# A decoder's first attention stage, with layer 0's values projected tile by tile inside the loop over heads instead of ahead of it

## The reference

```python
x = _layernorm(x + _L0_attn_ref(x, Wg, bg, Wv, bv, Wo, bo))
# in _L0_attn_ref, with H = 16 heads of 16 columns
g = x @ Wg.T + bg
v = x @ Wv.T + bv
attn = _genetic_fitness(g)          # cosine of g's rows, causal mask, fitness, softmax
out = einsum('bhij,bhjd->bhid', attn, v)
return out @ Wo.T + bo
```

## Time and profile before

| | us |
|---|---|
| median of 3 runs (lowest, highest) | 2650.11 (2647.54, 2652.91) |
| the profiled execution's own time | 2642.07 |
| its span | 2640.2 |
| first stage: projection, to its last VectorE operation | 0 to 79.8 |
| first stage: heads, first instruction to that of the next stage | 80.4 to 495.2 |

### The profile page before, as it was taken

How to read it: one execution, slowest core, us unless ns; L and a number is a source line. 1 busy time by engine, 2 the same in 40 slices (tenths; PEclk the granted TensorE clock), 3 DMA queues, 4 the chain that set the end, 5 groups by cost and what they waited for, 6 DMA issues and landing times. The chain is left out here.

```text
span 2640.2 us, 44590 instructions
## 1 busy us (share of the span) xinstructions
PE 2322.6 (88%) x17186; PEld 1783.3 (68%) x17186; DVE 1347.6 (51%) x2515; ACT 1131.5 (43%) x1934; POOL 845.9 (32%) x881
## 2 busy tenths in 40 slices
PE   9688888699998778698989869999999699999994
PEld 4567767466665555565666557888888588888893
DVE  5588878378887671002353536778778311111113
ACT  1466666355565554343333315555655111111113
POOL 2355545144444481000010113445444212212221
PEclk9699999799999898899999989999999799999997
DMA  2244435310120559574112031333332566665564
GB/s 76 79 103 121 122 102 131 92 33 25 31 67 17 182 195 225 128 210 136 32 32 64 24 130 54 111 113 101 99 120 91 216 203 181 180 198 173 183 223 140
DMA packets 212481, 313.23 MB, mean 119 GB/s; under 512 B 63792, under 2 KB 194736, under 8 KB 198960
## 3 DMA queue, kind: packets, MB, share of 16 engines
q1 hardware_dynamic: 190416, 255.25, 31.4%
q0 software_dynamic: 13440, 17.90, 3.7%
q10 hardware_dynamic: 8416, 37.23, 3.7%
HBM read 188.88 MB, written 121.45 MB: 118 GB/s over the span
## 5 line engine op out<-in xcount | busy, mean ns | idle before, releaser
L2653 ACT ACTIVATE me_h<-me_ps_h 128x512 f32<-128x512 f32 (+1 forms) x160 | 88.7, 554 | 423.8 <-PE me_ps_h L2631 423.8
L2694 DVE TENSOR_SCALAR me_yo<-me_ps_y,moe_xg 128x256 f32<-128x256 f32 x72 | 34.9, 484 | 422.8 <-PE me_ps_y L2641 369.1
L2567 POOL DMA_INDIRECT xo<-me_yo,me_row x72 | 112.7, 1565 | 410.2 <-DVE me_yo L2694 349.2
L2631 PE MATMUL me_ps_h<-me_xt,me_w 128*128 128x256 f32 (+1 forms) x1056 | 210.0, 357 | 0.0
L2641 PE MATMUL me_ps_y<-me_w,me_h 128*128 128x256 f32 x944 | 209.2, 379 | 0.7 <-DVE me_yo L2694 0.7
L2076 POOL TENSOR_TENSOR l1x_e<-l1x_e,l1x_ri 128x1024 f32<-128x1024 f32 x64 | 121.7, 1901 | 235.5 <-DVE l1x_ri L2360 235.5
L2641 PEld LDWEIGHTS me_ps_y<-me_w,me_h 128*128 128x128 f32 x944 | 179.0, 190 | 24.8 <-issue 1.1
L2631 PEld LDWEIGHTS me_ps_h<-me_xt,me_w 128*128 128x128 f32 x1056 | 182.0, 191 | 20.0
L664 POOL TENSOR_TENSOR l0x_e<-l0x_e,l0x_ri 128x1024 f32<-128x1024 f32 x64 | 120.0, 1896 | 202.7 <-DVE l0x_ri L893 202.7
L2195 PE MATMUL l1x_ps_p<-l1x_xct,l1x_w_q 128*128 128x256 f32 x512 | 122.3, 383 | 0.3 <-ACT l1x_xct L2281 0.3
L2233 PE MATMUL l1x_ps_o<-l1x_w_o,l1x_ot 128*128 128x256 f32 x512 | 118.8, 385 | 1.4 <-ACT l1x_ot L2306 1.4
(11 more groups left out here) (421 smaller groups left out, 5543.7 us busy)
## 6 DMA issues: line engine op xcount, KB each, us to landing
me_w<-in_w SPq DMA_DIRECT2D x33, 2048.0 KB, 9.6
xs<-dec_zero SPq DMA_DIRECT2D x31, 1032.0 KB, 6.9
k<-kv_kt ACTq DMA_DIRECT2D x16, 1024.0 KB, 6.4
v<-kv_va ACTq DMA_DIRECT2D x16, 1024.0 KB, 5.8
l1x_kt<-k SPq DMA_DIRECT2D x16, 1024.0 KB, 5.0
l1x_va<-v SPq DMA_DIRECT2D x16, 1024.0 KB, 5.7
moe_w_first<-in_w SPq DMA_DIRECT2D x7, 2048.0 KB, 9.9
moe_xg<-xs SPq DMA_DIRECT2D x32, 258.0 KB, 2.8
```

Of the source, the lines that this page charges most:

```text
L2567: pool.indirect_dma_start(token_rows, bass.IndirectOffsetOnAxis(row[:, j % 2, q:q + 1], 0), yo[:, j % 2, q, :], None, compute_op=ALU.add). ...
L2631: last = pe.matmul(ps_h[i % HB][:, f % 2, 0:P * size(j)], weights(j)[:, FFN * c + f * P:FFN * c + f * P + P], xt[:, j % 2, c, 0:P * size(j ...
L2653: act.activation(h[:, j % 2, 2 * i:2 * i + 2, 0:P * size(j)], ps_h[i % HB][:, :, 0:P * size(j)], ACT.Gelu).then_inc(gelued, 1)
```

## The change

The projection makes g alone: a product 256 columns wide (`ps_g`), and no v. x has four buffers instead of two. The reciprocal of the sums of squares is taken in four parts of eight tiles, three of them among the tiles; the logarithm comes ahead of the square root. The masks, the identity in bf16 and the padded tiles' memsets move from the start of the heads into the projection's block, where GpSimd and ScalarE do them ahead of the first tile.

The heads make v per tile. TensorE transposes x (`transpose_x`) and multiplies by Wv (`project_v`) in `ps_a[1]`, ScalarE copies between the two (`copy_xv`), VectorE adds the bias (`add_v`) into `va`, which now has four slots. The second half of the next tile's `transposes` waits for `add_v`, since both use `ps_a[1]`. The four weights and biases are waited for together. x has five slots, since `bias_x` moves two steps back; `roots` and `normalise` move one step back, and the lists of GpSimd and ScalarE are cut at another place. SP still stores tile n - 8 in its turn n.

```diff
 # l0_attn_project, VectorE and ScalarE
-                    dve.tensor_tensor(gv[:, n, :], ps_gv[n % 2][:, 0:D], bias[:, 0:D], ALU.add).then_inc(g_biased, 1)
-                    dve.tensor_tensor(va[:, n, :, 0:3:2, :],
...
+                    dve.tensor_tensor(gv[:, n, :], ps_g[n % 2][:, :], bias[:, :], ALU.add).then_inc(g_biased, 1)
...
+                def invert(k):
+                    at = slice(CHUNK * k, CHUNK * k + CHUNK)
+                    dve.wait_ge(summed, CHUNK * k + CHUNK)
+                    dve.tensor_scalar(lo[:, at, :], n2[:, at, :], 2.0 ** -115, None, ALU.max).then_inc(floored, 1)
+                    item_done(dve, floored, k)
+                    dve.reciprocal(inv[:, at, :], lo[:, at, :]).then_inc(inverted, 1)
...
-                unrolled(TILES, [(0, add_bias), (1, sum_squares)])
+                unrolled(TILES, [(0, add_bias), (1, sum_squares), (2, last_of_chunk)])
...
 # l0_attn_heads, SyncE
+                sp.dma_start(w_v[:, :, :], wgv.rearrange("(k p) n -> p k n", p=P)[:, :, D:2 * D]).then_inc(w_loaded, 16)
+                sp.dma_start(b_v[:, :], bcast(bgv[D:2 * D])).then_inc(w_loaded, 16)
...
-                    slot_free(sp, x_biased, n, 2)
-                    sp.dma_start(x[:, n % 2, :], x_in[n, :, :]).then_inc(x_loaded[n % 2], 16)
+                    slot_free(sp, x_biased, n, XR)
+                    slot_free(sp, xv_ready, n, XR)
+                    sp.dma_start(x[:, n % XR, :], x_in[n, :, :]).then_inc(x_loaded[n % XR], 16)
 # VectorE
+                def add_v(n):
...
+                    item_done(dve, v_ready, n)
+                    slot_free(dve, applied, n, VR)
+                    dve.tensor_tensor(va[:, n % VR, :, 0:3:2, :], ps_a[1][:, 2:4, :].rearrange("p a b -> p (a b)").rearrange("p (j a d) -> p j a d", a=2, d=HD),
...
 # TensorE
+                def transpose_x(n):
+                    item_done(pe, x_loaded[n % XR], n // XR, 16)
+                    item_done(pe, ops_copied, n, 2)
+                    slot_free(pe, v_biased, n, 1)
+                    for k in range(2):
+                        last = pe.transpose(ps_a[1][:, k, :], x[:, n % XR, k * P:(k + 1) * P], ident[:, :])
+                    last.then_inc(xv_ready, 1)
+
+                def project_v(n):
...
+                    item_done(pe, xv_copied, n)
+                    for k in range(2):
+                        last = pe.matmul(ps_a[1][:, 2:4, :].rearrange("p a b -> p (a b)"), xvt[:, n % 2, k * P:(k + 1) * P], w_v[:, k, :],
+                                         start=k == 0, stop=k == 1)
+                    last.then_inc(v_ready, 1)
...
+                            slot_free(pe, v_biased, n, 1)
 # ScalarE
+                def copy_xv(n):
+                    item_done(act, xv_ready, n)
+                    slot_free(act, v_ready, n, 2)
+                    act.activation(xvt[:, n % 2, :], ps_a[1][:, 0:2, :].rearrange("p a b -> p (a b)"), ACT.Copy).then_inc(xv_copied, 1)
...
-                walk([(0, copy_ops), (2, lambda n: exponentials(n, 1)), (0, lambda n: guard(n, 0)), (7, normalise), (2, copy_et), (0, lambda n: guard(n, 1)), (1, lambda n: exponentials(n, 0))])
+                walk([(8, normalise), (2, lambda n: exponentials(n, 1)), (0, lambda n: guard(n, 0)), (0, copy_xv), (2, copy_et), (0, lambda n: guard(n, 1)), (1, lambda n: exponentials(n, 0)), (-1, copy_ops)])
```

More of the change, by code:

```diff
@@ L225, in _ @@
                 identity_f32(nc, pool, ident, made)
+                pool.memset(after[:, :], 0.0).then_inc(cleared, 1)
+                pool.wait_ge(cleared, 1)
+                pool.affine_select(out=after[:, :], in_=after[:, :], compare_op=ALU.is_ge, fill=-1e30, base=0,
+                                   pattern=[[-1, P]], channel_multiplier=1).then_inc(after_cut, 1)
+                pool.memset(lpad[:, :, :, :], 0.0).then_inc(cleared, 1)
+                pool.memset(rpad[:, :, :, :], 0.0).then_inc(cleared, 1)
+                pool.wait_ge(cleared, 3)
+                pool.memset(lpad[:, :, :, HD + 1:HD + 2], 1.0).then_inc(one_set, 1)
+                pool.memset(rpad[:, :, :, HD:HD + 1], 1.0).then_inc(one_set, 1)
                 def square(n):
@@ L278, in l0_attn_heads @@
          applied, inverted, divided, multiplied, x_biased, residual_done, stats_done, mv_done, ln_step, ln_done, normed) = (kit.sem(n) for n in names)
[L279 removed]
+        x_loaded = [kit.sem(f"x_loaded{b}") for b in range(XR)]
         stored = [kit.sem(f"stored{t}") for t in range(G)]
@@ L303, in _ @@
                 pool.memset(on3[:, 1, :], 0.0).then_inc(parted, 1)
-                pool.memset(after[:, :], 0.0).then_inc(cleared, 1)
                 pool.memset(half[:, :], -0.5).then_inc(set_, 1)
@@ L444, in residual @@
                     dve.bn_aggr(mv[:, g % 2, t, :], stats[:, n % 2, :]).then_inc(mv_done, 1)
-                walk([(1, weigh_even), (0, lambda n: correlate(n, 1)), (2, divide), (0, row_sums), (2, residual), (-1, lambda n: correlate(n, 0)), (0, fitness)])
+                walk([(1, weigh_even), (0, add_v), (0, lambda n: correlate(n, 1)), (2, divide), (0, row_sums), (2, residual), (-1, lambda n: correlate(n, 0)), (0, fitness)])
             @block.tensor
             def _(pe):
-                pe.wait_ge(identb_set, 1)
-                pe.wait_ge(guard_set, 1)
                 pe.wait_ge(set_, 4)
+                def transpose_x(n):
[6 more added lines that the diff above has]
+                def project_v(n):
+                    if n == 0:
+                        pe.wait_ge(w_loaded, 64)
+                    item_done(pe, xv_copied, n)
[3 more added lines that the diff above has]
+                    last.then_inc(v_ready, 1)
                 def transposes(n):
@@ L527, in multiply @@
                     last.then_inc(multiplied, 1)
[L528 removed]
+                walk([(3, multiply), (0, transpose_x), (2, lambda n: transpose_e(n, 0)), (0, project_v), (2, lambda n: transpose_e(n, 1)), (1, sum_inverse), (2, lambda n: transpose_e(n, 2)), (2, lambda n: transpose_e(n, 3)), (0, lambda n: score(n, 1)), (2, apply), (-1, transposes), (-1, lambda n: score(n, 0))])
             @block.scalar
             def _(act):
[L532 to L534 removed]
+                def copy_xv(n):
+                    item_done(act, xv_ready, n)
+                    slot_free(act, v_ready, n, 2)
+                    act.activation(xvt[:, n % 2, :], ps_a[1][:, 0:2, :].rearrange("p a b -> p (a b)"), ACT.Copy).then_inc(xv_copied, 1)
                 def copy_ops(n):
```

132 lines of the change are left out of this document (67 added, 65 removed).

## The result

The changed kernel takes 2607.94 us (4 runs, 2606.00 to 2614.71), the kernel before on the same chip 2651.51 (2647.54 to 2654.84): ratio 0.9841, 95% interval 0.9818 to 0.9864. (The ratios here weigh all runs, so they are not quite the quotient of two medians; differences are those of the medians.) Two later comparisons gave 0.9838 [0.9815, 0.9861] and 0.9866 [0.9832, 0.9900], with medians 39.6 and 37.0 us apart. The profiled execution took 2609.12 us, its span is 2605.9.

A forecast was written before the change was run, and what follows sets the result against it. TensorE was taken to bound the projection; in the heads no engine was full and two chains closed the step. Terms -27.4 - 3.8 - 2.3 + 1 + 3 = -29.5 us, from the runs' median 2650.1, gave 2620.6; range 2611 to 2635.

The forecast's parts named there:

- The projection: Projection stage: tiles 1.08 us apart on TensorE with 256-column records, first product shorter, reciprocal parts costing 1; -27.4 us.
- The numbers for all tiles: Last addition to the heads' first instruction: reciprocal leaves the path, net one operation less; -3.8 us, bounds -3.3 and -4.2.
- The set-up: Start of the heads to TensorE's first transpose: memsets and mask move to the projection; -2.3 us, between 0 and -3.6.
- A full step: Each step of the heads: the new work on v fits under existing work; +0.04 us a step, +1 over 31.
- the product takes the place of the hole: Heads' step: `project_v` fills TensorE's idle time before 206.80, and the work between second and fourth quarter fits with 0.15 to spare.
- the two signs of being wrong in the steps: Heads: the prediction is wrong if a step exceeds 11.8 us, or if TensorE waits for `xvt`.
- The first steps: Heads' first three steps, at half clock: new work costs between 0 and 7.6 us, taken as +3.
- The pauses: Pauses without a releaser, as one of 2.95 us at 342.47: may come once more or less, 3 to 5 us.
- In part: Rival, heads: 0.2 to 0.9 us of the new 1.08 appear in each step; 2626 to 2648 us, chance 0.18.
- TensorE as the bound: Rival, heads: all 1.08 us are paid in each of 31 steps; 2653 us, no change, chance 0.04.
- the falling clock: Rival, projection: TensorE granted 1.2 GHz, 33 us more; 2654 us, no change, chance 0.03.
- late x: Rival, heads: x lands late behind the zeros, TensorE stands 2.4 us in each of 24 steps; 2678 us, chance 0.02.

## Why the prediction missed

**The projection, -27.4.** Measured -26.57. The additions were 1.08 us apart with the clock at 1.00, as worked out; the first of all (not among the lines above) came at 8.48 instead of 11.05 us, 2.6 sooner where 1.7 were counted, and the three parts of the reciprocal cost about 0.5 us each, where 1 in all was. **The numbers for all tiles, -3.8**: -3.94. **The set-up, -2.3**: -2.48. These three carried the forecast and were right.

**A full step, +0.04, +1 in all.** The step "the product takes the place of the hole" was right in kind and mis-sized: +0.19, about +5. The chain was the right one (`multiply`, `guard`, copy, product, second quarter). But in the heads four records of 256 columns follow each other in 0.97 us, not 0.86. In the changed kernel this is 196.90 - 195.93, and in before it stood between 204.59 and this row:

```profile
205.56 0.60 PE L498 MATMUL l0ah_ps_e<-l0a_ident,l0ah_e 128*128 128x128 f32 x4
```

And the copy lets the product start 1.82 us behind `multiply`, not 1.76: 0.06 + 0.11 = 0.17 more. The rate of another stage was taken for this one, though a row of this very product stood in the timeline. By the product made twice no cover is left: the next microsecond costs a microsecond. Of the two signs of being wrong in the steps, one did not come (a step over 11.8 us) and one did: TensorE waited for `xvt`. Its weight loads for the product did so 31 times between 50 and 470 us, for 10.0 us in all.

**The first steps, +3.** The two first profiles say -2.5, but over all profiled executions the stretch took 39.7 to 44.2 us with before's steps and 40.9 to 45.5 with the changed ones (without the doubled product), by when the clock rose and whether a pause fell in it. The term is small and its sign open.

**The pauses, "may come once more or less: 3 to 5 us, in the range", and "on the median of the runs, 8 us higher for the same program".** These are the step that failed, and they are one: pauses taken for an accident that both kernels share. In before they are no accident of 3 us. Eight places in the heads are exposed, each costs 2.4 to 5 us when it is hit, and moving them away is worth 15 to 18 us. The profiled execution had two such pauses, the second one with six had a span 10.2 us longer, and the 8 us by which the median lay over the profile were taken over to the changed kernel as they stood. The changed kernel has one or two pauses in its profiles, and its median lies 1.2 us under its profiled time. So of the 12.7 us between the forecast of 2620.6 and 2607.94, 8.0 + 1.2 = 9.2 are this step; the other 3.5 are the terms (profiled times 2642.07 - 2609.12 = 33.0 us apart, where 29.5 were forecast), and these hold the two pauses of before's profile too.

What took most of the pauses away, as the runs point to it, was in the change all along: its five slots of x and its new order send the zeros at another time in the step, away from TensorE's dense run. The forecast followed SyncE's order only to see whether x would be late. The new step of 357 instructions, by which the boundaries wander, is not needed for it, since the kernel without the work on v has 342 and no pause. What is left in the changed kernel falls on the zeros again, at 1473 and once at 11457.

How large this is stays rough. On one chip moving the boundaries gives 15.24 us in before and 9.56 in the changed kernel, so 5.7 by the medians and 7.8 by the means; resampling the runs puts the latter anywhere from 3 to 13. The earlier trace rows showed one pause; a second stood at 381.1 us and exactly 1024 instructions behind it, which the trace of before would have told.

**The sum.** With the pauses moved away in both kernels the change is worth 31.3 us on one chip (29.4 by the means), and 28.4 by two chips (2629.43 - 2601.02), where 29.5 were forecast. That it comes so near is in part luck, for the full step was 4 us worse than counted and the first steps some 5 better in the first profiles. Before's medians in the comparisons were 2651.51, 2646.79, 2647.03, 2642.70 and 2648.53. Its runs spread by 15 to 28 us within each of the later ones, a width that the pauses can make. What sets the level from chip to chip stays open.

**The rivals.** "In part" was true with 0.15 us a step, just under its 0.2. TensorE as the bound, the falling clock and late x did not come: x was waited for twice, 1.1 us in all.

## What to carry to other kernels

A pause that ends with nothing but "issue" deserves a count: number the instructions of its engine up to each pause, and if they agree modulo a block, the instruction fetch is late there. Two things have to meet for it: a block boundary at the end of a dense run, and a big transfer beside that run. A step whose length, times a small number, is near a multiple of that block puts the boundary at the same place of every such step; some instructions ahead move it away. Another order, or one more buffer, moves the transfer, and this can happen without being meant: so a change of slots or of a list's order is to be asked what it does to the big transfers. A product's time is to be taken from a row in the stage where it will stand, and when it fills a hole to the last tenth, the copy that feeds it should be started one instruction earlier.

## What was not expected of the hardware

Transfers of 16 KB on the instruction queue, one for each 256 instructions of TensorE, and pauses of up to 3.4 us at these boundaries. This chip's traces agree with the Trainium skill (Runtime: NRT & Kernel Launch, Instruction fetch mechanics) on blocks of 16 KiB, 256 instructions. It calls the crossing of a boundary mostly hidden, which most crossings here were; those at 193 or 194 modulo 256 at the end of a dense run, beside a DMA share of 0.6 to 1.1, often were not.

Behind most pauses of 2 us and more the granted clock is 0.50 for 3.4 to 10 us, and such a pause makes its step and the one behind it longer by 1.3 to 2.2 times its own length. And TensorE busy without a break up to 50.1 us did not keep the clock up: it fell at 52.5, behind 2.4 us of idle.
